# Layer 0's last four units: the second product whole behind both score pairs, and the pieces of other work side by side

## What is computed

```python
h = layernorm(x) * (1 + ca) + sa
x = x + ga * attention0(h)      # 16 heads of 8, all 2048 keys, softmax, output projection
h = layernorm(x) * (1 + cb) + sb
x = x + gb * (shared(h) + expert_sum(h))   # 16 experts, top 1, and one shared expert of width 512
# layer 1
x = x + ga * attention1(h)      # 8 query heads of 16, one key and value head, causal
x = x + gb * ffn1(h)            # r * (relu(k) ** 2 @ W_v), with the row before mixed in
# attention0
w = softmax(q @ k.T / sqrt(8)); out = (w @ v) @ Wo.T + bo
```

## Times and profile before

| | us |
|---|---|
| Median of three runs | 1150.22 (1148.53 to 1151.46) |
| The profiled execution | 1151.61 |
| Its span, first to last instruction | 1149.2 |
| PE busy in it | 1021.7 (89%) |
| DVE busy | 903.9 (79%) |
| ACT busy | 814.9 (71%) |
| POOL busy | 149.0 (13%) |
| Mean granted TensorE clock | 0.949 |

### The profile page before, as it was taken

The page is one execution under the profiler, slowest core; times in us unless marked ns, Lnnn a source line. Parts: engine busy times, 40 slices in busy tenths (PEclk is TensorE's granted clock), DMA queues, the critical chain, the costliest instruction groups (busy, mean ns, idle before and its releaser), DMA issues.

```text
span 1149.2 us, 22131 instructions
## 1 busy us (share of the span) xinstructions
PE 1021.7 (89%) x8766; PEld 349.2 (30%) x8766; DVE 903.9 (79%) x1154; ACT 814.9 (71%) x1556; POOL 149.0 (13%) x264
## 2 busy tenths in 40 slices
PE   4658999999999999999998999899978888798895
PEld 1212222222222222222232444343434443233323
DVE  5897999998999989999988777666766568587602
ACT  3105999998999998999976676567743555466683
POOL 2005000004000013000034000410121003000100
PEclk8658999999999999999999999999989999899997
DMA  4650400002000001000003431052003211200000
GB/s 105 128 98 17 137 2 2 2 2 44 1 2 2 2 21 23 2 1 3 2 2 116 122 87 31 27 93 49 1 1 111 74 57 28 38 10 2 10 1 9
DMA packets 47259, 42.04 MB, mean 37 GB/s; under 512 B 6102, under 2 KB 45366, under 8 KB 47158
## 3 DMA queue, kind: packets, MB, share of 16 engines
q1 hardware_dynamic: 44902, 35.27, 13.2%
q0 software_dynamic: 1824, 5.25, 1.6%
q10 hardware_dynamic: 432, 0.13, 0.0%
HBM read 26.83 MB, written 13.30 MB: 35 GB/s over the span
## 4 chain that ended last, share of the span: by engine, by line
PE 65%; DVE 21%; ACT 7%; issue 3%; DMA 2%; POOL 1%; SPq 1%; POOLq 0%; DVEq 0%; ACTq 0%
PE O L875 23%; DVE mx L1120 13%; PE T L846 12%; PE S L805 7%; PE S L812 4%; ACT PT L1351 3%; PE T L855 3%; PE S L961 2%; PE S L919 1%; PE S L929 1%; PE T L969 1%; PE S L920 1%; PE S L855 1%; PE T L884 1%; DVE Vf L1180 1%
## 5 line engine op out<-in xcount | busy, mean ns | idle before, releaser
L1120 DVE TENSOR_REDUCE mx<-S 128x2 f32<-128x1024 f32 (+2 forms) x672 | 757.0, 1179 | 89.2 <-PE S L812 38.2
L1351 ACT ACTIVATE PT<-T 128x512 f32<-128x512 f32 (+2 forms) x1280 | 675.8, 581 | 118.1 <-PE T L846 46.8
L875 PE MATMUL O<-PT,Va 128*9 128x256 f32 (+1 forms) x4040 | 319.0, 388 | 3.3 <-ACT Os L1358 3.3
L805 PE MATMUL S<-Ks,Qs 48*128 48x512 bf16 x1024 | 208.0, 397 | 26.3 <-DVE mx L1120 22.0
L846 PE MATMUL T<-Qs,Ks 51*128 51x512 bf16 x1024 | 202.1, 387 | 15.3 <-ACT PT L1351 7.2
L846 PEld LDWEIGHTS T<-Qs,Ks 51*128 51x128 bf16 x1024 | 55.6, 93 | 226.4 <-issue 131.9
L875 PEld LDWEIGHTS O<-PT,Va 128*9 128x9 f32 x4040 | 60.0, 88 | 207.4 <-issue 198.0
L812 PE MATMUL S<-K,Qs 96*128 96x512 bf16 (+3 forms) x320 | 85.5, 358 | 15.7 <-DMA Qs<-rows_q 5.4
L855 PE MATMUL T<-Qs,K 99*128 99x512 bf16 (+3 forms) x256 | 72.2, 350 | 7.7 <-ACT PT L1351 4.0
L875 PE MATMUL O<-PT,V 128*17 128x512 f32 (+3 forms) x640 | 75.0, 541 | 0.0
L805 PEld LDWEIGHTS S<-Ks,Qs 48*128 48x128 bf16 x1024 | 52.5, 95 | 53.4 <-DVE mx L1120 47.9
(11 more groups left out here) (225 smaller groups left out, 835.3 us busy)
## 6 DMA issues: line engine op xcount, KB each, us to landing
Qs<-in_L_ffn_experts SPq DMA_DIRECT2D x28, 192.0 KB, 2.7
Ks<-in_L_ffn_experts SPq DMA_DIRECT2D x20, 192.0 KB, 2.6
Qs<-rows_q SPq DMA_DIRECT2D x48, 64.0 KB
Vf<-sorted_x SPq DMA_DIRECT2D x12, 256.0 KB, 4.5
sorted_y<-Vf SPq DMA_DIRECT2D x12, 256.0 KB, 2.3
Qs<-rows_q SPq DMA_DIRECT2D x24, 128.0 KB, 4.6
rows_q<-q SPq DMA_DIRECT2D x7, 384.0 KB, 2.6
sorted_x<-XP POOLq DMA_DIRECT2D x1, 1792.0 KB, 10.8
```

Source lines behind the costliest of these rows:

```text
L805: m = e.matmul(two[:, i, :], Qs[r0:r0 + 48, hp, q0:q0 + 128], Ks[r0:r0 + 48, hp, CH * kb:CH * kb + CH], start=True, stop=True, tile_positi ...
L875: m = e.matmul(Ob[32 * g:32 * g + d1, lo:hi], v, PT[(2 * j + g // 2) % 4][:, p0 + lo:p0 + hi], start=(kt == 0 and halves[0] == 0), stop=Tr ...
L1120: e.tensor_reduce(mx[:, u % 2, h0:h0 + 2, kb], two[:, :, 0:n], AX.X, ALU.max).then_inc(free, 1)
L1351: e.activation(PT[(2 * j + pair) % 4][:, CH * i + lo:CH * i + CH], bank[:, lo:CH], ACT.Exp).then_inc(free, 1)
```

## The change

In steps 192 to 255 (layer 0, `u` from 12 to 15) a step is now emitted as: piece, `st` 0, both `s` pairs, `st` 1, whole `pv`, and behind it the light pieces and one more piece of other work, two more in unit 15. So the piece that stood in the middle of a step now stands at its end, next to the piece with which the next step begins. All other steps are as before, and each piece is emitted in the same step as before.

```diff
@@ -446,7 +446,18 @@
         k = rate(L, J)
         do_later()
         emit_st(J, 0)
-        if L == 0 and k:
+        if L == 0 and u >= 12:
+            for _ in range(min(k, 2)):
+                emit_s()
+            emit_st(J, 1)
+            for _ in range(k - 2):
+                emit_s()
+            emit_pv(J - LAG, (0, 1))
+            do_light(0.5)
+            do_later()
+            if u == 15:
+                do_later()
+        elif L == 0 and k:
             emit_s()
             emit_pv(J - LAG, (0,))
             do_light(0.5)
```

## The result

The changed kernel takes 1181.94 us (median of four, 1179.87 to 1182.41); the kernel before, run beside it, 1150.60 (1148.53 to 1151.46). The ratio is 1.0267, 95% interval 1.0249 to 1.0285: slower, by 31.3 us where 27.2 were forecast. The profiled execution took 1182.41, its span is 1180.7.

What follows compares the result with a forecast made beforehand. PE was taken to bound all four stretches, its waits counting whole in the second; stretch terms 7.9 + 16.8 + 4.5 - 2.0 = +27.2 us on the median 1150.22 gave 1177.4 us, range 1160 to 1190.

Steps and rivals of the forecast that it cites:

- The latency of the exponential: Plain steps: st 1 must wait until 1.17 us after st 0, so a step takes 2.47, 0.21 more than 2.26.
- The rival that counted on PE's saving: Steps 192 to 255: PE's saving counts and the waits don't, giving 1137 us; chance 0.06.
- Stretch 1: Steps 192 to 217, 86.11 us before: +7.9 us from plain steps and waits behind each up (bounds +3 to +12).
- the forecast 1.34: Steps behind an up in stretch 1: st 1 starts at 2.51 instead of 1.17 us, 1.34 more in each of four.
- Stretch 2: Steps 218 to 232, the expert tiles, 64.78 us before: +16.8 us (bounds +8 to +25).
- seven turns forecast at 5.85: Steps 218, 219, 228 to 232: m2 waits for m1's chain, 5.85 us instead of 4.41, 10.1 in all.
- five turns forecast at 5.36: Steps 222 to 226: s 1 waits for m1's S bank, 5.36 us a turn, 0.95 more each, 4.8 in all.
- Covered exactly, 1.62: Expert tiles before: a half step of 1.09 and m0 of 0.53 exactly cover m1's chain of 1.62 us.
- Stretch 3: Steps 233 to 241, 55.06 us before: +4.5 us (+1 to +7), with -0.5 in 233 to 235.
- Stretch 4: Steps 242 to 255: layer 1's scores give st 1 enough work ahead, so -2.0 us (-3 to 0).
- The rival of the clock: Expert steps: PE falls to its lower clock level behind the new waits, another 10 us, 1188; chance 0.17.
- The rival in which the waits fall where PE would wait anyway: Steps 192 to 241: slack takes up new waits, the experts' loss halves, ending near 1150 to 1158 us; chance 0.07.

Runs made afterwards that it cites:

- Number 9: Changed kernel with layer 0's exponentials of units 12 to 15 cut to the first 256 of 512 columns; one run, 1173.05 us.
- number 10: Changed kernel with the two matmuls of s 1 issued three times in steps of units 12 to 15 with two layer 0 score pairs; ratio 1.0383.
- number 2: Kernel before with only the middle piece moved to the step's end, product in halves and score pairs apart; ratio 1.0179, median 1180.23 us.
- number 8: Changed kernel with the light pieces (no matmul) emitted between s 0 and s 1 instead of at the step's end; ratio 1.0259.
- number 5: Kernel before with all due pieces side by side at the start of steps 218 to 232, product still in halves; ratio 0.9953, 1144.54 us against 1149.88.
- Number 12: Changed kernel with steps 233 to 242 emitted as in the kernel before; ratio 1.0208.

## Why the prediction was right, step by step

**The latency of the exponential: right.** The forecast step was 2.47 and the measured one is 2.47. Number 9 shows that the 1.16 is the exponential's, number 10 that PE's work isn't in it, number 2 that with the halves back the step is 2.26 again. (Whole product and paired scores were only ever taken back together.) The rival that counted on PE's saving put its point of decision at `st` 1 less than 0.9 behind `st` 0; it came at 1.16 wherever nothing else delayed it. The two halves of the advice in the Trainium skill, Perfetto Trace Analysis, section Matmuls, which the prediction named, came out so: the product whole is indeed cheaper on PE (0.98 against 1.10), and the latency between two uses of a bank cost more than it saved.

**The sum, +27.2 for a measured +31.3: near, but in part by luck.** The four stretches together lost 34.35 us, and layer 1 gave 3.13 back. The granted clock of the four was 0.98, 1.00, 0.97 and 0.96 and is 0.93, 0.96, 0.92 and 0.93. Length times what the clock lacks to 1 is 5 us before and 18 now. (The mean over the whole span, 0.949 and 0.950, hides this: the unchanged part ahead of step 192 had 0.94 before and 0.95 now, at equal length.) If that is what the lower level costs in the four stretches, which is an estimate (single steps with a fall took 1.5 to 1.7 more than the same step without), the waits and the work alone made some 21 us, by stretch about 4.9, 12.2, 4.1 and 0, where the forecast had 7.9, 16.8, 4.5 and -2.0; and 13 us are the clock's, which the forecast's sum had at nothing. Terms set too high and a term left out nearly met. The parts:

**Stretch 1, +9.85 for +7.9: the terms were off, the sum was near by luck.** Steps 192 to 203 lost 2.40, 0.20 each, as said. Further on, 214 to 217 lost 0.28 together where 0.21 each was forecast: `st` 1 came 1.16 behind `st` 0 there too, but it had come 1.09 to 1.15 behind before, and a piece can take less at the step's end (`m0` 0.38, where it took 0.56 between a product and `st` before). The three ups after 204 cost what was forecast where they stand clean (`st` 1 at 2.53 in steps 210 and 213, 2.51 forecast); with falls of the clock among them they came to +1.94, +1.83 and +0.65, and step 211 to +1.38. Step 209 gave 2.60 back in this execution, and took 1.9 more than before in the other one; the -1 set against it had no fixed thing behind it.

*The step that failed is step 204*, +3.35. The prediction said that each piece keeps its step, and looked for what the piece no longer covers. It did not ask what the light pieces, which have no matmul, were moved past. The routing chain on DVE stood behind one maximum before and behind two now, and its last instruction met one of POOL, whose own list had not changed (last section). ACT's list puts `half_score`, which waits for that chain, ahead of the instruction that empties `up`'s bank. This adds 1.4 to the forecast 1.34 (`st` 1 at 3.90, and at 2.50 in number 8, which takes it away); the rest of the step's loss is a fall of the clock, which number 8 has too.

**Stretch 2, +15.44 for +16.8: right in kind, two terms mis-sized.** Six of the seven turns forecast at 5.85 are 5.79, and one is 7.40: 11.24 for 10.1. The three others lost 2.48 for 1.9, of which 1.57 is a fall of the clock in step 220 (0.9 without it). The five turns forecast at 5.36 are 4.75: 1.72 for 4.8. The prediction priced the three pieces at 0.53, 0.61 and 1.09. Side by side they take 0.27, 0.45 and 0.99, 0.52 less. The 0.26 of `m0` was no work at all: its neighbours are the same in number 5, where it takes 0.28. "Covered exactly, 1.62" in the prediction was a wait. In every turn `m2` started 1.62 behind the end of `m1`, with `m0` ahead of it or not, and 0.15 behind the end of DVE's second instruction (703.23, and 707.64):

```profile
702.66 0.42 DVE L1241 TENSOR_TENSOR Vf<-S,Vf 128x256 f32<-128x256 f32 x1
```

Where `m0` stood there the wait was too short to be printed as idle. The other 0.16 and 0.10 come from the neighbours of `m2` and `m1` (last section). In the five turns the chain was 1.52 to `s` 1 (679.46 to 680.98) for 1.62, the remaining 0.10. Number 5 shows the pieces' part of this: 0.30 of the 0.52 arrives, the rest goes into the two short waits named there.

**Stretch 3, +7.49 for +4.5: the term left out is the clock.** Steps 237 to 241 lost 3.49, where 5.0 was forecast (4.3, and 2 less 1.3). The waits for the exponentials behind ACT's copies are there, up to 1.68, and show more than was set for them; step 240 gave 1.67 back, since PE ran at the lower level in it before and not now. In the second execution it did not give it back. Steps 233 to 235 lost 4.00 where -0.5 was forecast. Two `up` side by side were taken to cost one release. They cost both, since the second's instruction on ACT waits for the first's last one on DVE (both add into `Vf`):

```profile
755.98 0.39 PE L816 MATMUL S<-Ks,Qs 48*128 48x512 bf16 x2 [0.20 <-DVE Vf L1195]
...
756.01 0.60 ACT L1412 ACTIVATE Vf<-S 128x512 f32<-128x512 f32 x1 [1.64 <-DVE Vf L1195]
...
758.22 0.39 PE L816 MATMUL S<-Ks,Qs 48*128 48x512 bf16 x2 [1.85 <-DVE Vf L1195]
```

But the waits of these steps add up to 4.1 (0.17, 1.85, 0.20 and 1.85), and to 4.1 in the kernel before (1.14 twice, 1.15 and 0.67). So they are not the loss. Steps 233 and 234 in the profile of the changed kernel, and in its second execution (columns as above):

```profile
738.23:745.80 7.57, 7.23 (x27) 2.12 (x26) 3.24 (x4) 3.09 (x6) 3.56 (x4) 0.77 0.22 61
745.80:755.39 9.59, 7.57 (x26) 2.42 (x26) 4.99 (x7) 3.26 (x6) 7.15 (x9) 0.82 0.18 49
741.46:747.56 6.10, 5.76 (x26) 1.89 (x26) 3.24 (x4) 3.08 (x6) 2.40 (x3) 1.00 0.18 54
747.56:755.50 7.94, 5.93 (x27) 1.95 (x26) 5.00 (x7) 3.26 (x6) 6.11 (x7) 1.00 0.23 58
```

At a clock of 1.00 steps 233 and 234 take 6.10 and 7.94, against 7.22 and 8.43 before. Step 235 took 9.70 at a clock of 0.82, and 9.72 at 0.82 in the second execution; every profile of this order has a fall of the clock there. With 1.6 for it the three steps come to 0.7 less than before, by this estimate, close to the forecast -0.5. The account of the releases was wrong, but cheaper neighbours made up for it, and what the sum lacked was three falls of the clock. Number 12 shows that they belong to the order of these steps: with it taken back the clock is 0.97 again.

**Stretch 4, +1.57 for -2.0.** Steps 243 to 255 gave 1.3 back, near the forecast. *The step that failed is 242*, +2.89, about half of it a fall of the clock (the whole product took 1.82 in it, for 0.98). The copy of layer 1's values empties the T bank that `st` 1 wants, and on DVE it stands behind all that `down` sets off: three additions into the rows and their statistics, 3.5 us from 800.09 on:

```profile
800.78 0.39 PE L857 MATMUL T<-Qs,Ks 51*128 51x512 bf16 x2
...
803.54 0.19 DVE L1265 COPY V<-T 128x64 f32<-128x64 f32 x1
...
803.79 0.39 PE L857 MATMUL T<-Qs,Ks 51*128 51x512 bf16 x2 [2.04 <-DVE V L1265]
```

The forecast looked at the exponentials ahead of `st` 1 in each step, and took it that with layer 1's scores between there was enough. It did not look at who empties the third T bank. The chain is as long in the kernel before; but there a pair and a product stood between `down` and the values' piece, and now the two stand next to each other ahead of the step.

**The rival of the clock, chance 0.17, came in good part.** It set another 10 us, all in the experts' stretch. The estimate above is 13 us over the four stretches, some 3 of them in the experts'. I don't add this to the terms above, since it is inside them: the steps named with a fall of the clock contain it. What it was built on was misread in one place: behind the waits of 1.14 PE did stay at the upper level, but these were three in 8 us (717.96 to 726.40) and a fourth of 0.67, not four in 17. The clock is also what the profiles show between the ratios of 1.027 and 1.035.

The rival in which the waits fall where PE would wait anyway came true in steps 214 to 217 alone, and even there for a part of the wait only.

## What to carry to other kernels

Before pulling the work of a tight loop together, write down for each buffer the time from its filling to its release (here 1.16 for a T bank, 1.5 to 1.6 behind `m1`, 2.3 behind `up`) and what PE has to do in between; where that work goes elsewhere, the difference is the price. Look at the pieces without a matmul too, and at each engine's list from the view of whoever waits for it: both steps that were missed here (204 and 242) were a DVE or ACT instruction for which PE waited behind another chain. Before a step's loss is given to a wait, compare the step in two executions and look at its granted clock: the losses of steps 233 to 235 here were falls of the clock. And a group whose start keeps the same distance from another engine's chain in every turn is waiting, even where no idle time is printed; moving just those pieces together, with the attention left in halves, was the version that gained.

## What the runs showed of the hardware

The cast of 128 x 64 numbers from fp32 to bf16 on DVE (`OHb`) takes 0.20 us, but 1.16 where an element-wise instruction of POOL on 128 x 512 had started 0.15 before it. It stands four times in each of the 14 profiles. In the ten in which POOL's instruction had just started it took 1.16 and ended 0.04 to 0.05 behind that instruction (600.20 and 600.15 in the changed kernel); in the other 46 places POOL had nothing under way and it took 0.19 to 0.20. The Trainium skill describes this in SBUF — State Buffer, section "SBUF: two separate sides": DVE and GpSimd share a port pair, and of a GpSimd instruction and a DVE one of the kinds that need the pair, whichever starts first keeps it until its end while the other blocks. The trace agrees, with an instruction of 64 columns held for 0.96 us. Not every DVE instruction is held: L1191 on 128 x 512 took 0.69 beside POOL's next one in step 204 (601.03, POOL from 600.23 to 601.50), as it did in number 8 with none on 128 x 512 under way. No run here moved POOL's instruction by itself.

PE's idle times of 0.34 a step brought no fall of the clock in steps 192 to 203. In the experts' stretch, between waits of 1.33, the two orders without them (number 10, where repeated matmuls fill them, and number 2, where the halves do) had a clock of 1.00 in place of 0.92 to 0.98. These are two profiles against six, so it is an observation and not a proof. Why the same program falls to the lower level in other steps from one execution to the next stays open.

A group of fp32 matmuls on the whole array is cheaper by about 0.1 us for each neighbour of its own kind. `m0` takes 0.38 between a product and `st` (654.80 to 655.18 in the changed kernel) and 0.27 with `m2` behind it. `m1` takes 1.09 between two of attention's groups and 0.99 with `m0` behind or `m2` ahead of it. `m2` takes 0.61 with `st` behind it, 0.54 between a product and an `up` (706.51 to 707.05 in number 5) and 0.45 with such groups on both sides. Where it took 0.61 it had also waited for DVE, so that part of its difference is not settled.
